# A two-deep software pipeline on one core: two units of work leave the tiles for the mixed stretch, and a hardware loop is written out

## The reference, cut to what matters

```python
adj_d = jnp.where(rem, 0.0, adj_)
vals = jnp.where(nd[..., None], x[:, None, :, :], jnp.inf)
s = jnp.sort(vals, axis=2)
nv = nd.sum(2)
for tau, w in zip(TAUS, WTS):                    # 0.25, 0.5, 0.75
    pos = tau * jnp.maximum(nv - 1, 0)
    lo, hi = floor(pos), ceil(pos)
    agg = agg + w * (v_lo + frac * (v_hi - v_lo))   # s taken at lo and hi
h = relu((x + agg) @ W1 + b1); y = (h @ W2 + b2) * mask
```

## Time and profile before

| | |
|---|---|
| Time of three runs | 3703.91 us median (3702.68 to 3704.35) |
| The profiled execution | 3705.9 us by the device, span 3704.1 us |
| PE busy | 2640.1 us (71%) |
| DVE busy | 3181.8 us (86%) |
| ACT busy | 1946.7 us (53%) |
| Granted TensorE clock, mean | 0.822 of full |

### The profile page before, as it was taken

One profiled execution on the slowest core, in us unless ns is written; L12 is line 12 of the kernel. 1 busy time (PEld: TensorE's weight loads), 2 busy tenths in 40 slices (PEclk: granted clock), 3 DMA queues, 4 the chain that ended last, 5 costly groups with the idle time before them and its releaser, 6 DMA issues. The chain is left out here.

```text
span 3704.1 us, 48769 instructions
## 1 busy us (share of the span) xinstructions
PE 2640.1 (71%) x17098; PEld 1201.0 (32%) x17098; DVE 3181.8 (86%) x5858; ACT 1946.7 (53%) x2672; POOL 8.0 (0%) x21
## 2 busy tenths in 40 slices
PE   0000144888888888888788888787888888887896
PEld 0000022333333333333333333333333333333665
DVE  8999989888988989898989898989898888855676
ACT  2114443656656565656565656565656666553232
POOL 0000000000000000000000000000000000000000
PEclk6555576988989988989898989898989889888777
DMA  1001000333232323232322323232322232332011
GB/s 37 0 0 57 6 0 21 54 53 54 43 55 44 57 39 58 41 57 41 57 40 55 44 53 60 35 60 38 57 49 53 47 55 42 43 63 44 33 34 34
DMA packets 242849, 158.50 MB, mean 43 GB/s; under 512 B 126504, under 2 KB 228026, under 8 KB 242362
## 3 DMA queue, kind: packets, MB, share of 16 engines
q1 hardware_dynamic: 238490, 154.49, 23.7%
q10 hardware_dynamic: 4128, 1.05, 0.2%
HBM read 40.14 MB, written 14.70 MB: 15 GB/s over the span
## 5 line engine op out<-in xcount | busy, mean ns | idle before, releaser
L1006 ACT ACTIVATE hot<-bcast,consts 128x1024 bf16<-128x1024 f32 x744 | 829.5, 1115 | 498.5 <-PE bcast L567 497.8
L580 PE MATMUL rows<-hot,table 128*64 128x512 bf16 x4608 | 734.9, 430 | 112.7 <-DVE prod L1394 110.3
L1394 DVE SCALAR_TENSOR_TENSOR prod<-near,consts,rows 128x512 f32<-128x512 bf16 x768 | 561.2, 744 | 263.6 <-PE rows L580 210.6
L554 PE MATMUL ring<-member,neigh_t 128*128 128x512 bf16 x2048 | 542.7, 405 | 75.6 <-ACT words L967 50.2
L589 PE MATMUL found_bank<-prod,consts 128*64 128x512 f32 x1536 | 428.9, 635 | 4.9 <-DVE prod L1394 4.9
L567 PE MATMUL bcast<-idx_t,consts 32*128 32x512 f16 x1488 | 317.2, 417 | 111.8 <-ACT hot L1006 110.7
L580 PEld LDWEIGHTS rows<-hot,table 128*64 128x64 bf16 x4608 | 226.8, 116 | 408.9 <-issue 300.7
L554 PEld LDWEIGHTS ring<-member,neigh_t 128*128 128x128 bf16 x2048 | 182.1, 102 | 422.4 <-issue 121.6
L492 PE MATMUL ring<-identb,adj_b 128*128 128x128 bf16 x256 | 35.4, 272 | 366.6 <-ACT adj_b L894 354.0
L567 PEld LDWEIGHTS bcast<-idx_t,consts 32*128 32x128 f16 x1488 | 73.0, 92 | 455.6 <-ACT hot L1006 302.1
L967 ACT ACTIVATE words<-ring 128x512 uint16<-128x512 f32 x256 | 146.8, 594 | 136.0 <-PE ring L554 135.5
(11 more groups left out here) (332 smaller groups left out, 4323.0 us busy)
## 6 DMA issues: line engine op xcount, KB each, us to landing
near<-idx_bt SPq DMA_DIRECT2D x768, 128.0 KB
late<-in_adj_dram SPq DMA_DIRECT2D x16, 1024.0 KB, 5.5
adjt_d<-late SPq DMA_DIRECT2D x16, 512.0 KB, 2.7
adj_l<-adjt_d SPq DMA_DIRECT2D x16, 512.0 KB, 6.0
adj_s<-adjt_d SPq DMA_DIRECT2D x16, 512.0 KB, 3.7
parts_d<-parts SPq DMA_DIRECT2D x6, 512.0 KB, 5.1
table<-parts_d SPq DMA_DIRECT2D x192, 16.0 KB, 2.2
out_dram<-x_all SPq DMA_DIRECT2D x4, 512.0 KB, 3.8
```

What stands on the lines that cost most here:

```text
L554: ins = mm(ring[u % 2][:, :], kept_t[:, j, P * i:P * i + P], member[:, j, n // 2, 512 * (n % 2):512 * (n % 2) + 512], start=(j == 0), stop ...
L580: ins = mm(rows[u % 2][C * h:C * h + C, :], table[:, s, GROUPS * h + g8, :], hot[:, u % HOT, h, :], start=(s == 0), stop=(s == 2))
L1006: run(hot[:, u % HOT].rearrange(flat), spread_bank(l, u)[0][:, 0:2, :].rearrange(flat), ACT.Relu, bias=eq_bias[:, :]).then_inc(S["hot_read ...
L1394: stt(out=prod[:, u % DEEP, :], in0=near[:, u % NEAR, :], scalar=iota_b[:, :], in1=rows[u % 2][:, :], op0=ALU.is_equal, op1=ALU.mult).then ...
```

## The change

Three constants are changed, and a loop. The second and third tile (`PLACES[1]`, `PLACES[2]`) lose their unit at place 9, the one after the last fold; the fourth has its first unit at place 2 in place of 1. `LATE` falls from 24 to 22. The steps of the mixed stretch are moved so that it takes 26 units in place of 24: between `bits_start` and `members(p, 0)` there are two units in place of one, and between `ffn_end` and `clear_own` two in place of one; all other gaps between DVE's parts hold as many as before. The loop over the last stages, on all four engines, is a Python loop, so its three (SP: four) rounds stand in the program one after the other, with constants where registers were.

```diff
-PLACES = ((6, 7, 8), (1, 4, 5, 6, 8, 9), (3, 4, 5, 6, 8, 9), (1, 3, 4, 5, 6, 7, 7, 8, 9))
+PLACES = ((6, 7, 8), (1, 4, 5, 6, 8), (3, 4, 5, 6, 8), (2, 3, 4, 5, 6, 7, 7, 8, 9))
...
-STEP = [LATE + n for n in (0, 1, 2, 4, 5, 6, 8, 10, 12, 13, 14, 16, 18, 20, 22, 24)]
+STEP = [LATE + n for n in (0, 2, 3, 5, 7, 8, 10, 12, 14, 15, 16, 18, 20, 22, 24, 26)]
...
-            with sp.Fori(0, B // SLOTS) as g0:
+            for g0 in range(B // SLOTS):
...
-            with pe.Fori(1, B // SLOTS) as g0:
+            for g0 in range(1, B // SLOTS):
...
-            with act.Fori(1, B // SLOTS) as g0:
+            for g0 in range(1, B // SLOTS):
...
-            with dve.Fori(1, B // SLOTS) as g0:
+            for g0 in range(1, B // SLOTS):
```

## The result

The changed kernel takes 3716.71 us (median of 17 runs, 3707.14 to 3723.64), the kernel before 3703.86 us beside it (17 runs, 3702.68 to 3705.99). The ratio is 1.0033, with a 95% interval of 1.0026 to 1.0040: slower by 0.33%. The profiled execution has a span of 3713.9 us, 9.8 more than the 3704.1 before.

What follows compares the result with a forecast made beforehand. DVE was taken to bound the mixed stretch, while losing time to others in the tiles; 19 + 2 - 2 - 0.3 = +19 us against 3703.91 gave 3723 us, 0.5% slower, range 3690 to 3743.

Steps and rivals of the forecast that it cites:

- Tiles, -4.2 us per pass: Tiles 2 to 4: PE hands over 4.2 us early; bounds 2.7 to 5.7, the latter without half clock (1.2 GHz).
- over 5 us: Sign that the forecast is wrong: tiles 2 to 4 together shorter by over 5 us, where some 4 was expected.
- The first pair, +1.74: Start of mixed stretch: second unit's late lookup puts everything behind it 0.67 + 1.07 = 1.74 us later; bounds 0.67 to 2.4.
- U28, 0.7 + 2.5 + 0.6 = 3.8: Second unit between `ffn_end` and `clear_own`: 0.7 us for it, 2.5 waiting for its near load, 0.6 before the next unit.
- that chain keeps its place on DVE's axis: Mixed stretch: PE's lookup ahead of the turn, ACT's L907 and SP's store stay put; the near load issues at 1801.77.
- The sum of a pass: A pass with a store: -4.2 + 1.74 + 3.8 = +1.3 us; 14 of them, +19.
- First pass: First pass with a store: no `ffn_end`, some 2.3 us of DVE work, so its wait is longer: +2 in the total.
- last selecting pass: The pass that prepares no next graph: -4.2 + 1.7 + 0.7 = -2 us.
- Last stages, -0.3: Last stages: the loop costs at most 0.5 us in three rounds; taken as -0.3 us, bounds -2 and +2.
- The load is in time: Rival: near load of LATE + 6 lands by 1804.2, a pass gives -1.8 us, 3677 us; chance 0.17, in time or nearly.
- PE gives more back: Rival: tiles gain 5.7 us a pass, not 4.2; 3701 us, no change; chance 0.18 shared with nothing but the loop.
- The other two: Rivals: tiles gain only 2.7 us, 3745 us, chance 0.15; nothing but the loop changes, 3703 us, within a shared 0.18.

Runs made afterwards that it cites:

- three edits: Near loads up to LATE+7 ahead of the store, totals behind the turn, ACT's hot rows ahead of the root: changed kernel 0.9863; kernel before, loops written out, 0.9994.
- that of one unit: The change, but tile 3 keeps its unit and the mixed stretch gets one unit, not two: 3713.22 us, 1.0021 of the kernel before.

## Why the prediction was right, and where its terms were off

The forecast was 3723 us, slower; it was 3716.71, slower. The place and kind of the new cost were right, and the gain in the tiles was real. By its steps:

- **Tiles, -4.2 us per pass.** Measured -5.7 (61.39 for 67.10 us): the end of the range that the prediction tied to a tile 3 without its piece of half clock, and it is gone (1.00 where the earlier trace rows have 0.92). By the prediction's own sign ("over 5 us") this term was wrong, and the step that failed is the assumption that this piece stays. Nor was 5.7 a clear gain for the pass: in the kernel before, the passes without this piece have tile 3 1.5 us shorter and the mixed stretch about as much longer. L1428 of tile 3 waits for ACT as foreseen (28 such waits, not 14). Counted from the start of tile 2, it comes 2.4 us earlier (24.30 us for 26.70), where the prediction had 2.3. The move in tile 4 gives nothing, as one experiment showed. The line of L1428, from the timeline of DVE in the changed kernel:

```profile
1748.91 0.43 DVE L1428 TENSOR_SCALAR late<-late 128x1024 uint16<-128x1024 uint16 x1 [1.06 <-ACT late L967]
```

- **The first pair, +1.74.** Measured +1.72 in the mean of passes 2 to 14: from L1499 to L1310, the first operation behind the pair, DVE takes 4.37 us for 2.65.
- **U28, 0.7 + 2.5 + 0.6 = 3.8.** Measured 5.4: from L1594 to L1598, where the unit stands, DVE takes 7.91 us for 2.55 in the same mean, with waits of 3.9 and 0.9 in it. The price of a load was right (4.83 us and 2.10 more, for 4.6 and 2.15). The step "that chain keeps its place on DVE's axis" was wrong: the order of units changed which of them is odd, and put the totals ahead of the turn. With the totals behind it the wait is the predicted one. What lies behind L1598 in the mixed stretch took 0.6 us less (65.37 for 66.01).
- **The sum of a pass** was +1.3 and measured +0.9: one error of 1.5 us in the tiles, one of 0.9 in the mixed stretch (+6.45 for +5.54), of opposite sign. That the forecast came out nearer than its terms is luck.
- **First pass** +3.4 for +3.3; **last selecting pass** -2.5 for -2.
- **Last stages, -0.3.** Measured -2.8, and -3.0 with the loops alone: more than the bound of -2. The term looked at one wait of DVE at one round's end, and at nothing inside a round (there 1.29 us for 1.12).
- **The rule of the Trainium skill** weighed there ("DMA: Bandwidth & Descriptors", "Anatomy of one DMA") is a fit for DMAs issued from GpSimd. An estimate by it has the load landed in 2.3 us. The trace shows 4.83 us from issue to use, and does not agree, for SP's queue and this transfer.
- **The rivals.** "The load is in time" priced a pass without that wait at 3677 us; the kernel that takes the wait away by loading earlier takes 0.9925 of the time before, 3676 us on the prediction's scale. The sum is near, its terms are not: tiles 2 to 4 give 5.9 us there and the mixed stretch costs 3.5. "PE gives more back" was true of its mechanism, but the longer wait ate it. The other two did not come.

Open: why the runs of the changed kernel spread over 16 us where those of before spread over 3. Its passes, of 176.7 to 180.8 us, differ in the clock granted in tiles 1 and 4 and at the head of the mixed stretch, but that this makes the spread was not shown.

## What to carry to other kernels

Work moved out of a stretch bound by one engine must be followed through every queue it now passes: here the units were cheap on DVE, and the cost lay in SP's order of a store and two loads, and behind it in ACT's order. A wait that is taken away uncovers the next one on the chain, so look at what the waiting had covered; three edits that are worth nothing in the kernel before (0.9994) turn this change from 1.0033 into 0.9863. A sum made at one granted clock can miss in a stretch and still hold for the pass. And where an engine does something for every second unit, shifting a step by one unit puts that work on its other side.

## What the runs showed of the hardware

- A near load of 128 KB issued on SP's queue behind a 512 KB store is used 4.83 us after its issue, the next 2.10 us later. Two of these loads issued ahead of the store cost nothing that can be measured where no unit waits for them (1.0001).
- Matmuls of one lookup take 1.50 us at the lower clock (1803.94) and 0.84 at the higher one (1807.74 in the same pass). A change in a tile's order can move the stretch at the lower clock to another tile. It costs that tile 1.3 to 1.6 us (22.9 for 21.6, 20.4 for 18.8, 24.86 for 23.22) and the pass much less: 0.3 us in the kernel before, 0.4 in that of one unit.
- Three rounds of a loop on four engines (four on SP) cost 3.0 us in the last stages against the same instructions written out, 1 us a round, where DVE's wait ahead of L1782 at a round's end shows only 0.68. From L1768 to L1795 inside a round it is 1.29 us for 1.12.
